# The sums' bank joins the scores' one step later, and batch 0's side work in the last unit moves and stays in PSUM

## The reference, cut to what matters

```python
q = _qdq(x) @ _qdq(wq).T + bq          # x here: layernorm of the input
k, v = split(cond @ wkv.T + bkv)       # cond: 4 x 1601 x 512
attn = softmax(einsum('bnhd,bmhd->bhnm', q, k) * scale)   # 16 heads of 32
o = einsum('bhnm,bmhd->bnhd', attn, v)
out = _qdq(o) @ _qdq(wp).T + bp        # _qdq: scale by the row's maximum, round, clip
x = x + out
h = _layernorm(x)                      # goes into the feed-forward net
```

## Time and profile before

| what | value |
| --- | --- |
| median of 3 runs (lowest, highest) | 2742.91 us (2737.63, 2744.13) |
| the profiled execution's own time | 2743.92 us |
| its span in the trace | 2742.1 us |
| PE busy / DVE / ACT / POOL | 93% / 67% / 45% / 47% of the span |
| attention 0 | from 640 to 1446 us of the span |
| last unit of attention 0 | from 1374.76 to about 1445 us |

### The profile page before, as it was taken

How to read it: one execution, slowest core, us unless ns; L and a number is a source line. 1 busy time by engine, 2 the same in 40 slices (tenths; PEclk the granted TensorE clock), 3 DMA queues, 4 the chain that set the end, 5 groups by cost and what they waited for, 6 DMA issues and landing times. The chain is left out here.

```text
span 2742.1 us, 34009 instructions
## 1 busy us (share of the span) xinstructions
PE 2544.5 (93%) x13272; PEld 1642.9 (60%) x13272; DVE 1824.8 (67%) x2486; ACT 1241.8 (45%) x1869; POOL 1292.0 (47%) x337
## 2 busy tenths in 40 slices
PE   8999999998999999999978999997899999996898
PEld 8888888885444444444426777786333333333776
DVE  5554544456676676766774766554899899986764
ACT  3222312213656566665642222222788888872211
POOL 1000000004999999999950000000799999994210
PEclk9999999999999999999999999999999999998999
DMA  8777766565534535335106635436977777773200
GB/s 295 236 237 252 257 231 247 180 193 117 113 78 85 107 64 111 80 83 108 63 4 226 223 120 180 142 121 164 201 163 161 156 156 157 160 211 87 78 31 31
DMA packets 218434, 405.11 MB, mean 148 GB/s; under 512 B 18169, under 2 KB 93977, under 8 KB 218209
## 3 DMA queue, kind: packets, MB, share of 16 engines
q1 hardware_dynamic: 218272, 402.93, 53.1%
HBM read 260.63 MB, written 140.59 MB: 146 GB/s over the span
## 5 line engine op out<-in xcount | busy, mean ns | idle before, releaser
L1335 POOL TENSOR_TENSOR pooled<-pooled,probs 128x2048 f32<-128x2048 f32 x140 | 640.8, 4577 | 22.0 <-ACT probs L1209 2.3
L1209 ACT ACTIVATE probs<-psum 128x512 f32<-128x512 f32 (+1 forms) x832 | 459.2, 598 | 373.6 <-PE psum L1106 370.5
L1236 DVE TENSOR_REDUCE win_max<-psum 128x1 f32<-128x802 f32 x480 | 453.8, 987 | 169.7 <-PE psum L1071 169.5
L2014 DVE TENSOR_SCALAR probs<-psum,bound 128x1024 f32<-128x1024 f32 (+1 forms) x416 | 499.0, 1274 | 52.5 <-PE psum L1931 52.5
L1981 ACT ACTIVATE probs<-probs 128x1024 f32<-128x1024 f32 (+1 forms) x416 | 437.1, 1058 | 104.1 <-DVE probs L2014 62.1
L2040 POOL TENSOR_TENSOR pooled<-pooled,probs 128x2048 f32<-128x2048 f32 x94 | 432.9, 4606 | 35.8 <-ACT probs L1981 25.1
L1106 PE MATMUL psum<-q_st,k_st 128*128 128x512 f32 (+1 forms) x832 | 337.0, 439 | 36.0 <-ACT den_sb L1221 17.9
L250 POOL TENSOR_TENSOR r_q<-ve_q,minus_half 128x4 f32<-128x4 f32 x8 | 9.1, 1134 | 667.0 <-DVE ve_q L210 667.0
L1106 PEld LDWEIGHTS psum<-q_st,k_st 128*128 128x128 f32 (+1 forms) x832 | 149.5, 186 | 258.5 <-ACT probs L1209 175.1
L1071 PE MATMUL psum<-k_st,q_st 96*128 96x402 f32 x960 | 266.7, 359 | 6.3 <-DVE o_sb L1267 5.1
L1931 PE MATMUL psum<-q_st,k_st 128*128 128x512 f32 (+1 forms) x832 | 253.1, 434 | 12.3 <-PEq L175 10.4
(11 more groups left out here) (252 smaller groups left out, 4295.9 us busy)
## 6 DMA issues: line engine op xcount, KB each, us to landing
k_st<-k_hi SPq DMA_DIRECT2D x64, 801.0 KB, 11.8
k_st<-k_lo SPq DMA_DIRECT2D x48, 801.0 KB, 11.3
k_hi<-kt_hi SPq DMA_DIRECT2D x32, 801.0 KB, 4.1
k_lo<-kt_lo SPq DMA_DIRECT2D x32, 801.0 KB, 6.0
v_rows<-v_out SPq DMA_DIRECT2D x96, 256.0 KB
v_st<-v_rows SPq DMA_DIRECT2D x24, 768.0 KB
q_st<-q_hi SPq DMA_DIRECT2D x64, 256.0 KB, 10.5
w<-w_hi_d SPq DMA_DIRECT2D x64, 256.0 KB, 3.0
```

The costliest lines, as they stand in the source:

```text
L1209: A.activation(probs[i % NPROBS][0:rows, j, :], bank(score_banks.where["score", u, t, j])[0:rows, :], ACT.Exp, scale=1.0 / ROOT).then_inc( ...
L1236: V.tensor_reduce(win_max[:, r, j, c:c + 1], window(windows.where["max", u, i])[:, :, 0:MV], AX.XY, ALU.max).then_inc(max_done, 1)
L1335: G.tensor_tensor(pooled[u % 2][:], before[:], probs[tile(u, k) % NPROBS][:], ALU.add).then_inc(pool_added, 1)
L2014: V.tensor_scalar(probs[i % NPROBS][0:rows, half * W:half * W + W, :], window(("score", u, t, half))[0:rows], bound[0:rows, u // NG, t:t + 1],
```

## The change

Four edits, all in `attention_0`:

1. `three_banks` begins with step 5 in place of 4.
2. In the last unit, `first_codes` goes from step 0 to step 3, and `first_projection` with `first_rows` from step 2 to step 5. The norm goes with `first_rows` (before, it stood behind step 4's closing).
3. `first_rows` works in place in the projection's windows in PSUM: scale PSUM to PSUM, add the bias PSUM and SBUF to PSUM, add to the rows PSUM and SBUF to SBUF. The windows come free with the third operation (`y_done`), not the first.
4. `root_on_pool` stands behind all of POOL's additions.

```diff
-            LAST_SUM = 1
+            LAST_SUM, CODES_AT, ROWS_AT = 1, 3, 5
                 def three_banks(u, t):
-                    return 4 <= t < pooled_tiles(u) + LAG
+                    return 5 <= t < pooled_tiles(u) + LAG
                             m.then_inc(y_ps, 1)
-                            windows.freed_by(y_read, 2 * half + 2)
+                            windows.freed_by(y_done, 2 * half + 2)
-                            if now == (UNITS - 1, 0):
+                            if now == (UNITS - 1, CODES_AT):
                                 first_codes()
-                            if now == (UNITS - 1, 2):
+                            if now == (UNITS - 1, ROWS_AT):
                                 first_projection()
...
-                            y = first.y[r % 2]
-                            if r >= 2:
-                                V.wait_ge(y_done, r - 1)
-                            V.scalar_tensor_tensor(out=y[:], in0=window(windows.where["first", r // 2])[:, r % 2, :],
-                                                   scalar=first.step[:, r:r + 1], in1=first.w_row[:], op0=ALU.mult,
-                                                   op1=ALU.mult).then_inc(y_read, 1)
-                            V.wait_ge(y_read, r + 1)
-                            s = own.after(V.tensor_tensor(y[:], y[:], first.bp[:], ALU.add))
+                            y = window(windows.where["first", r // 2])[:, r % 2, :]
+                            s = own.after(V.scalar_tensor_tensor(out=y, in0=y, scalar=first.step[:, r:r + 1],
+                                                                 in1=first.w_row[:], op0=ALU.mult, op1=ALU.mult))
                             V.wait_ge(own.sem, s)
-                            V.tensor_tensor(first.rows[:, r, :], first.rows[:, r, :], y[:], ALU.add).then_inc(y_done, 1)
+                            s = own.after(V.tensor_tensor(y, y, first.bp[:], ALU.add))
+                            V.wait_ge(own.sem, s)
+                            V.tensor_tensor(first.rows[:, r, :], y, first.rows[:, r, :], ALU.add).then_inc(y_done, 1)
...
-                        if now == (UNITS - 1, 0):
+                        if now == (UNITS - 1, CODES_AT):
                             first_codes()
-                        if now == (UNITS - 1, 2):
+                        if now == (UNITS - 1, ROWS_AT):
                             first_rows()
-                        if now == (UNITS - 1, CLOSE_AT):
                             V.wait_ge(y_done, RT)
                             for _ in norm_on_dve(own, nm, first.rows, first.cols, 0, normed):
...
-                            if u == UNITS - 1 and k == pooled_tiles(u) - 2:
-                                root_on_pool(nm, 0)
+                    root_on_pool(nm, 0)
```

More of the change, by code:

```diff
@@ L1011, in attention_0 @@
                 o_coded, q_ps, q_turned = sem("o_coded"), sem("q_ps"), sem("q_turned")
-                y_ps, y_read, y_done, normed = sem("y_ps"), sem("y_read"), sem("y_done"), sem("normed")
+                y_ps, y_done, normed = sem("y_ps"), sem("y_done"), sem("normed")
                 score_banks, windows = Banks((0, 1, 7)), Banks((1, 2))
```

## The result

The changed kernel takes 2726.8 us (median of 5 runs, 2725.49 to 2728.72) where the kernel before took 2743.08 (5 runs, 2737.63 to 2747.22): ratio 0.9942, 95% interval 0.9927 to 0.9956. That is 16.3 us less; the forecast was 2722, in a range of 2708 to 2732. The profiled execution took 2728.02 us, its span is 2726.2.

What follows compares the result with a forecast made beforehand. In attention 0, PE's order with ACT's hand-overs sets a unit's length, POOL next, 2 us below. Gains 15.4 + 3.1 - 0.1 + 2.3 = 20.7 us from 2743.9, less 1.0 for the median: 2722 us, range 2708 to 2732.

Steps and rivals of the forecast that it cites:

- The bank in the plain units: Attention 0's plain units: leaving bank 7 out of step 4 gains 15.4 + 3.1 us, with 0.1 off for unit 0.
- The step 4 term: Step 4 of units 1 to 14: S(4,0) no longer waits for ACT's copy, 1.10 us each, 15.4 us.
- The term of the boundary: Between units up to unit 14: the turned bank rotation starts S(0,1) 0.22 us earlier, 14 times, 3.1 us.
- What is late next: Step 4 of plain units: S(4,1) does not wait; followers put at 0, bounds 0 and 1.13 us a unit.
- the bank gives half: Rival, plain units: part of the 1.10 us returns at S(4,2) or step 0; 18.4 becomes 9.2, 2731 us; 10%.
- the wait moves: Rival: the bank's gain is given back in the same step, last unit level; sum 0 to 5, 2740 us; 6%.
- the slower one: Rival, step 4: ACT's copy stands ahead of the exponentials, both score pairs wait; + 10.9 us, 2754; 4%.
- The codes: Last unit, after step 3: codes ready at 26.1, PE there at 14.5, so PE waits 11.7 us, against 8.07 before.
- The alternation: Last unit: DVE's quantiser operations and POOL's additions take turns, one instruction each; first three products pass between additions, codes at 26.1.
- the free codes: Rival, last unit: all six quantiser operations pass, PE waits for nothing; last unit gains 15.5, sum 33.9, 2709 us; 12%.
- the single run: Rival, last unit: products pass as one run, only the two passes meet additions; PE waits 7.2 us, 2718 us; 13%.
- The last unit: Attention 0's last unit: 14.4 removed, less 11.7 for codes and 0.9 for two-bank waits, plus 0.5: 2.3 us gained.

Runs made afterwards that it cites:

- after_again: The changed kernel traced once more, no edit: 2724.95 us, ratio 0.9930 to the kernel before.
- pool_waits: The changed kernel with POOL's first addition of the last unit held until the codes are made: 2712.02 us, ratio 0.9881 to the kernel before.
- codes_psum: The changed kernel with the quantiser's products and first pass writing to idle PSUM banks, the last pass reading there: 2709.72 us, ratio 0.9876 to the kernel before.
- rows_sbuf: The changed kernel with edit 3 undone, batch 0's rows going through SBUF as before: 2725.13 us, ratio 0.9933 to the kernel before.
- bank_only: The kernel before with edit 1 alone (three banks from step 5), side work as before: 2730.07 us, ratio 0.9946.
- no_move: The changed kernel with edit 2 undone (side work at its early place), all else kept: 2722.46 us, ratio 0.9919 to the kernel before.
- side_only: The changed kernel without edit 1 (three banks from step 4 again), edits 2 to 4 kept: 2741.1 us, ratio 0.9988 to the kernel before.

## Why the prediction was right, point by point

- **The bank in the plain units (forecast 15.4 + 3.1 - 0.1 = 18.4).** The plain units took 734.2 us before and 717.4 after: 16.9 gained (17.4 in after_again). The step 4 term measured 1.10, as forecast. The term of the boundary was mis-sized: S(0,1) came 0.22 us earlier, but it now runs behind a wait of 0.34 us and takes 0.50 in place of 0.40, so only 0.14 reached the values (from the values of step 12 to those of the next unit's step 0 it is 3.54 us before, 3.40 after):

```profile
1310.26 1.07 PE L1118 MATMUL psum<-probs,v_st 128*32 128x512 f32 x8
...
1312.87 0.50 PE L1106 MATMUL psum<-q_st,k_st 128*128 128x512 f32 x1 [0.34 <-ACT probs L1209]
...
1313.66 1.07 PE L1118 MATMUL psum<-probs,v_st 128*32 128x512 f32 x8
```

14 x 1.24 - 0.1 = 17.3. The seven traces with edit 1 give between 16.6 and 17.5.

- **What is late next: nothing.** In unit 14's step 4 L1106 doesn't wait for an exponential at all, and step 4 to 5 kept its length. Unit 14 lasts 47.84 us (47.7 forecast), and POOL's idle time fell to 0.78 us (0.8 forecast). The rivals in which the bank gives half, in which the wait moves, and the slower one are ruled out: the values of step 4 come 4.45 us after those of step 3, as between the two-bank steps 1 and 2 of unit 14 in the kernel before (4.46).
- **The codes (forecast: 11.7 us late).** 10.94 and 10.96 us in the two traces, just under the 11 to 12 that I gave as a sign. The alternation went as worked out: one product through for each addition, the fourth behind addition 3, then the two passes. PE came to the codes at 14.6 (14.5 forecast), and they were ready at 25.4 (26.1), with the zero 0.92 us ahead of the last unit's first value matmul, as S(0,0) stood before: I had allowed some 0.3 us too much for each of the gaps between additions (three additions took 14.0 us, 4.67 each). The 18.71 us of the four products rule out both rivals about the codes, the free codes and the single run; pool_waits and codes_psum show that the turns with POOL are the cause, and their price: 12.9 us.
- **What the alternation rested on.** I had read more into the earlier trace rows than they hold. The POOL row shown there begins at 2508.66, when the second of DVE's two additions is nearly through. This is the one between them, with the first of the two additions and ACT's work for the second:

```profile
2506.49 1.08 DVE L2298 TENSOR_TENSOR o_lo<-o_cols,o_hi 128x512 fp32r<-128x512 f32 x1 [3.07 <-ACT o_hi L2247]
2506.99 1.71 POOL L2413 TENSOR_TENSOR o_cols<-o_cols,o_rec 128x512 f32<-128x512 f32 x1
2507.06 0.63 ACT L2247 ACTIVATE o_hi<-o_cols 128x512 fp32r<-128x512 f32 x1 [0.59 <-POOL o_cols L2413]
```

The two additions had something between them: each waits for ACT's `o_hi`, and the second's was ready at 2507.69, when the first had ended (2507.57). So this pair says nothing on DVE instructions that follow each other without a wait. That such a pair alternates with POOL too was a guess; the changed kernel's trace is the first to show it. It came true, and the 11.7 us rest on it; so far that term was luck as much as reading.

- **The last unit (forecast 2.3).** 68.4 us before, 65.5 and 66.9 after: 2.9 and 1.5. The wait for the codes was 0.8 shorter than forecast; in after_again the longer half clock behind it, which the sum has no term for, took 1.4.
- **Edit 3 and edit 4 (forecast 0).** In the new forms the DVE additions took 0.70 and 0.69 us each beside POOL's additions 4 to 6, the lower bound, and the rows 8.6 us in all. That agrees with the rule of the Trainium skill ("SBUF — State Buffer", Who interferes with whom) that a DVE instruction with at most one SBUF input, outside the two-port modes, does not contend with GpSimd. rows_sbuf shows that this is worth nothing in the changed kernel. The norm ended 15 us ahead of the last closing.
- **The sum.** 20.7 forecast, 19.8 and 19.0 in attention 0's two traces. In the first, 1.5 too much in the plain units and 0.6 too little in the last unit offset each other in part. The median came 16.3 lower in the first comparison and 19.6 in the second. No run shows the cause of that difference; the other stages' scatter from trace to trace is as large.

What I had not seen is that edits 2 and 3 do the same work. In the order in which the prediction adds the edits up, its booking holds: with edit 1, the move and the late root, the rows still in SBUF (rows_sbuf), the last unit takes 66.7 us, 1.7 less than before (2.3 forecast) and 3.7 less than in bank_only, and the rows in PSUM then add nothing. But the rows in PSUM remove the wait for the window without the move as well: no_move takes 64.0. On top of them the move costs 2.1 us by that one trace, since it lets POOL's additions start under the quantiser: edit 2, which I had counted as a gain, is none in the kernel as changed. The wait for the copy (1.43), booked under edit 2, goes by edit 1: in bank_only it is gone too. A small slip besides: eight values at half clock and as much again for the scores are 1.8 us, not 1.9.

Timeline of DVE in the changed kernel, the first rows and the last closing:

```profile
1396.97 0.70 DVE L1288 TENSOR_TENSOR psum<-psum,o_bp 128x512 f32<-128x512 f32 x1
1397.70 0.69 DVE L1290 TENSOR_TENSOR f_rows<-psum,f_rows 128x512 f32<-128x512 f32 x1
...
1426.75 0.26 DVE L1263 RECIPROCAL rec<-psum 128x16 f32<-128x16 f32 x1 [15.01 <-PE psum L1092]
```

## What to carry to other kernels

A stall of TensorE can be what keeps another engine's work apart from yours: before moving the stalled work to a later place, look at what will now run during it, here POOL's additions under DVE's quantiser. Where DVE's operations take turns with POOL's, as the SBUF to SBUF ones did here, count each of them as one POOL instruction (4.7 us here) while POOL has work queued, however short they are; then hold POOL back for the few microseconds the chain needs, or take the chain through idle PSUM banks. And in this rotation of buffers, the one that was handed over late was better left out for one more step than waited for.

## What the runs showed that I had not expected

- Strict alternation holds for DVE instructions with no wait between them: four products of 0.4 us took 18.71 us beside the rest of one addition and three whole ones, and in side_only each of the two passes took 4.2 us more than alone.
- The three PSUM forms didn't meet POOL: writing PSUM from an SBUF input, PSUM to PSUM, and PSUM to SBUF took 0.68, 2.30 and 2.29 us with POOL adding beside them and none waited. For 128x2048 that is 1.9 times the 1.23 us of the SBUF form, and still the cheaper way here.
- Executions differ by up to 3.5 us in a single stage whose instructions are the same (projections 639.2 to 642.7), while attention 0 repeated within 0.9 us in two pairs of traces. A part of a change worth 2 us can be read from its stage and not from the total.
